# Retention and feed-forward block: the states gathered right behind the scores, their share added right behind the own values, into other PSUM banks

## The reference, cut to what matters

```python
xn = _layernorm(x)
# attention: 8 heads of 16, chunks of 64 tokens, in every chunk
attn = einsum('bhid,bhjd->bhij', qc, kc) * D          # D: causal, with decay
o_intra = einsum('bhij,bhje->bhie', attn, vc)         # a block's own values
o_inter = einsum('bhid,bhde->bhie', qc * decay_q, S)  # the states' share
S_new = decay_s * S + einsum('bhjd,bhje->bhde', kc * decay_k, vc)
# feed forward: ternary weights and a low-rank part
h = _bitlinear(xn, w_fc) + gate * (xn @ v.T @ fast_b.T @ u.T)
r = maximum(h, 0)
out = x + o @ Wo + _bitlinear(r * r, w_proj)
```

## Time and profile before

| | us |
|---|---|
| median of 3 runs | 129.81 |
| lowest, highest | 127.7, 129.81 |
| the profiled execution's own time | 129.01 |
| its span, first to last instruction | 127.0 |
| outside the span | 2.0 |
| PE busy | 117.0 (92%) |
| DVE busy | 99.2 (78%) |
| ACT busy | 78.7 (62%) |
| POOL busy | 64.0 (50%) |

### The profile page before, as it was taken

The page is one execution under the profiler, slowest core; times in us unless marked ns, Lnnn a source line. Parts: engine busy times, 40 slices in busy tenths (PEclk is TensorE's granted clock), DMA queues, the critical chain, the costliest instruction groups (busy, mean ns, idle before and its releaser), DMA issues.

```text
span 127.0 us, 6564 instructions
## 1 busy us (share of the span) xinstructions
PE 117.0 (92%) x2860; PEld 92.8 (73%) x2860; DVE 99.2 (78%) x261; ACT 78.7 (62%) x158; POOL 64.0 (50%) x60
## 2 busy tenths in 40 slices
PE   4979999988999999499999999999999999499991
PEld 4425869856688778377788778878897889377890
DVE  0788795489799969858699979896999799729832
ACT  3265669967871897227972897188738774382910
POOL 7099803984439161923439252916193529544400
PEclk9999999999999999999999999999999999999998
DMA  3849920000023000400023001300020002000202
GB/s 105 296 149 320 389 92 34 0 3 5 8 90 81 5 0 23 145 7 0 0 92 74 0 0 53 112 0 0 0 83 0 0 0 83 0 5 0 88 5 83
DMA packets 3357, 7.71 MB, mean 61 GB/s; under 512 B 384, under 2 KB 896, under 8 KB 3216
## 3 DMA queue, kind: packets, MB, share of 16 engines
q1 hardware_dynamic: 2880, 7.01, 16.3%
q10 hardware_dynamic: 464, 0.50, 1.2%
HBM read 5.42 MB, written 2.10 MB: 59 GB/s over the span
## 4 chain that ended last, share of the span: by engine, by line
PE 80%; DVE 10%; issue 4%; ACT 2%; POOL 1%; DVEq 0%; POOLq 0%
PE ps_work L659 10%; PE ps_score L735 8%; PE ps_work L663 7%; PE ps_work L660 7%; PE ps_score L705 6%; PE ps_score L747 5%; PE ps_score L781 5%; PE ps_y L761 4%; PE ps_y L762 4%; PE ps_score L720 3%; DVE sums_of L532 3%; PE ps_turn L668 3%; PE ps_y L765 2%; DVE xn L491 2%; PE ps_turn L692 1%
## 5 line engine op out<-in xcount | busy, mean ns | idle before, releaser
L300 POOL TENSOR_TENSOR sq_lo<-square,sq_hi 128x512 fp32r<-128x512 f32 x31 | 39.8, 1295 | 36.2 <-ACT sq_hi L356 36.2
L347 ACT ACTIVATE square<-ps_work 128x512 f32<-128x512 f32 x32 | 19.1, 596 | 23.1 <-PE ps_work L663 22.6
L516 DVE TENSOR_TENSOR scores<-ps_score,cst 128x512 f32<-128x512 f32 x32 | 20.3, 682 | 1.6 <-PE ps_score L705 1.6
L305 POOL TENSOR_TENSOR q_pair<-q_dec,cst 128x1024 f32<-128x1024 f32 x7 | 13.3, 1894 | 15.9 <-DVE q_dec L501 15.9
L356 ACT ACTIVATE sq_hi<-square 128x512 fp32r<-128x512 f32 x32 | 20.1, 627 | 0.1
L352 ACT ACTIVATE square<-square 128x512 f32<-128x512 f32 x32 | 18.9, 630 | 0.1
L491 DVE TENSOR_SCALAR xn<-x_in,mean_var,rstd 128x128 f32<-128x128 f32 x32 | 14.9, 528 | 0.3
L659 PE MATMUL ps_work<-xn_hi,w_hi 128*128 128x512 f32 x32 | 14.3, 447 | 0.4 <-issue 0.4
L735 PE MATMUL ps_score<-scores,v_pad 64*32 64x64 f32 x1024 | 12.5, 225 | 1.6 <-issue 1.6
L663 PE MATMUL ps_work<-xn_lo,w_hi 128*128 128x512 f32 x32 | 12.6, 394 | 0.0
L660 PE MATMUL ps_work<-xn_hi,w_lo 128*128 128x512 f32 x32 | 12.6, 393 | 0.0
(11 more groups left out here) (123 smaller groups left out, 238.6 us busy)
## 6 DMA issues: line engine op xcount, KB each, us to landing
x_in<-x_tok SPq DMA_DIRECT2D x8, 256.0 KB, 3.4
resid<-x_feat SPq DMA_DIRECT2D x1, 2048.0 KB, 7.7
out_feat<-resid SPq DMA_DIRECT2D x7, 256.0 KB
po_in<-ffn_weights SPq DMA_DIRECT2D x1, 320.0 KB, 3.2
fc_in<-ffn_weights SPq DMA_DIRECT2D x1, 256.0 KB, 3.7
q_table<-q_decay SPq DMA_DIRECT2D x1, 256.0 KB, 3.5
wqvk<-qvk_weights ACTq DMA_DIRECT2D x1, 192.0 KB, 3.9
cst<-const ACTq DMA_DIRECT2D x1, 129.0 KB, 3.9
```

Source lines behind the costliest of these rows:

```text
L300: nc.gpsimd.tensor_tensor(sq_lo[p][:, f, :], square[p][:, f, :], sq_hi[p][:, f, :].bitcast(F32), ALU.subtract).then_inc(lo_ready, 1)
L347: nc.scalar.activation(square[b.parity][:, f, :], ps_work[f % 2][:], ACT.Relu).then_inc(relu_ready, 1)
L516: nc.vector.tensor_tensor(scores[:, g].rearrange("p t s i -> p (t s) i"), ps_score[:, g].rearrange("p (a i) -> p a i", i=BLK), causal.unsq ...
```

## The change

- The banks `ps_turn` and `ps_y` become one tensor `ps_both`, and `gather_states` writes its states there (row block r to bank r) and not to banks 2 and 3 of `ps_score`. It waits no longer for masks, and stands right behind `score`. So `take_states` must have read `ps_both` before the transposes of the next batch (`turn_xn`) write there.
- `carry(b)` moves to the end of its own batch's pass, right behind `own_values(b)`.
- `hidden` runs tiles 0, 1 and 2, then scores and states, then tile 3. `second_product(before)` moves behind the transposes.
- VectorE: `low_o(before)` comes first; the masks are taken in order, with `take_states` behind the first; the three adds stand behind `low_xn` and ahead of `finish(before)`. The statistics of the batch after next are made at the end of a pass.
- ScalarE: `high_o(before)` first, other order of relu, square and rounded square, the root of the batch after next last. GpSimd: the four subtractions in a row, then `spread_q`.
- In the last batch the subtraction of the fourth tile goes from VectorE to GpSimd.
- `place_program` adds tiny products on small tiles: 40 at the start in place of 12, 9 ahead of the first `carry`, 20 ahead of the last own values in place of 6. Of the three wide products at the start one and a half are left.

The diff, cut to its core:

```diff
+        ps_both = pb("ps_both", [P, ROWS, SEQ])
+        ps_turn, ps_y = ps_both[:, 0, :], ps_both[:, 1, :]
+        w1_bank = ps_score[:, NG - 1, :]
...
             def body(b):
-                for f in range(2):
+                for f in range(NF):
                     low_square(b, f)
                 spread_q(b.step(1))
-                for f in range(2, NF):
-                    low_square(b, f)
...
-            def body(b):
+            def body(b, more):
+                high_o(b.step(-1))
                 take_relu(b, 0)
                 take_relu(b, 1)
-                root(b.step(1))
+                take_relu(b, 2)
                 take_square(b, 0)
+                high_square(b, 0)
                 take_square(b, 1)
-                high_square(b, 0)
-                high_o(b.step(-1))
-                take_relu(b, 2)
+                take_relu(b, 3)
+                round_xn(b.step(1))
                 high_square(b, 1)
-                round_xn(b.step(1))
-                take_relu(b, 3)
                 take_square(b, 2)
+                high_square(b, 2)
                 take_square(b, 3)
-                high_square(b, 2)
+                high_square(b, 3)
                 copy_k(b.step(1))
                 copy_k_tok(b.step(1), 0)
-                high_square(b, 3)
                 copy_k_tok(b.step(1), 1)
+                if more:
+                    root(b.step(2))
...
-            def body(b):
-                before, after = b.step(-1), b.step(1)
-                statistics(after)
-                statistics_done(after)
-                take_states(before)
-                variance(after)
-                for k in range(3):
-                    add_states(before, k)
+            def body(b, more):
+                before, after, later = b.step(-1), b.step(1), b.step(2)
+                low_o(before)
                 for step in range(4):
                     inverse_root(after, step)
                 normalise(after)
-                low_o(before)
+                mask_scores(b, 0)
+                take_states(b)
+                for g in range(1, NG):
+                    mask_scores(b, g)
                 low_xn(after)
-                for g in MASK_ORDER[:2]:
-                    mask_scores(b, g)
+                for k in range(3):
+                    add_states(b, k)
                 finish(before, ps_y)
                 decay_q(after)
...
             def turn_xn(b, before=None):
                 pe.wait_ge(xn_ready, b.count(1, 1))
+                if before is not None:
+
+                    pe.wait_ge(state_step, before.count(3, 1))
...
-                pe.wait_ge(scores_ready, b.count(NG, ROWS))
+                pe.wait_ge(v_ready, b.count(2, 2))
...
-                            ins = mm(ps_score[g * GW:(g + 1) * GW, ROWS + r, t * GW:(t + 1) * GW],
+                            ins = mm(ps_both[g * GW:(g + 1) * GW, r, t * GW:(t + 1) * GW],
...
+            def hidden_and_scores(b):
 
                 pe.wait_ge(q_ready, b.count(1, 1))
                 hidden(b, 0)
                 pe.wait_ge(k_ready, b.count(1, 1))
                 hidden(b, 1)
+                hidden(b, 2)
+                pe.wait_ge(o_lo_ready, b.count(1, 0))
+                score(b)
+                gather_states(b)
+                hidden(b, 3)
+
+            def body(b):
+                before, after = b.step(-1), b.step(1)
+                hidden_and_scores(b)
+                turn_xn(after, b)
                 second_product(before, ps_y, range(NF))
-                carry(before)
-                hidden(b, 2)
-                hidden(b, 3)
-                turn_xn(after)
-                pe.wait_ge(o_lo_ready, before.count(1, 1))
-                score(b)
                 output_product(before, ps_y)
                 project_q(after, b)
                 project_k(after, b)
                 project_vk(after, 0)
                 project_vk(after, 1)
-                gather_states(b)
                 own_values(b)
+                carry(b)
```

More of the change, by code:

```diff
@@ L85, in over_batches, with over_middle @@
         body(Batch(half, 2))
+def over_middle(engine, body):
+    with engine.Fori(0, NB // 2 - 2) as half:
+        body(Batch(half, 1), True)
+        body(Batch(half, 2), True)
+    body(Batch(NB // 2 - 2, 1), True)
+    body(Batch(NB // 2 - 2, 2), False)
 def build(nc, x_tok, x_feat, qvk_weights, ffn_weights, rank_weights, const, q_decay, out_feat):
@@ L586, in _ @@
             normalise(after)
-            for g in MASK_ORDER:
-                mask_scores(first, g)
             dve.wait_ge(proj_step, 1)
@@ L594, in _ @@
             nc.vector.tensor_scalar(wo_scaled[:], wo_in, inv_scale2[:], None, ALU.mult).then_inc(wo_ready, 1)
+            mask_scores(first, 0)
+            take_states(first)
+            mask_scores(first, 1)
+            mask_scores(first, 2)
             low_xn(after)
+            mask_scores(first, 3)
             decay_q(after)
@@ L683, in project_vk @@
             def project_vk(b, side):
-                if side == 1 and b is first:
-                    pe.wait_ge(q_ready, b.count(1, 1))
-                elif side == 1:
+                if side == 1 and b is not first:
                     pe.wait_ge(y_free, b.count(1, 0))
@@ L803, in _ @@
             project_vk(first, 1)
-            score(first)
-            after = first.step(1)
-            pe.wait_ge(v_ready, 2)
-            pe.wait_ge(w1_split, 1)
-            for f in range(NF):
-                hidden(first, f)
-            turn_xn(after)
+            after = first.step(1)
+            pe.wait_ge(q_ready, 1)
+            pe.wait_ge(w1_split, 1)
+            hidden(first, 0)
+            pe.wait_ge(k_ready, 1)
+            hidden(first, 1)
+            hidden(first, 2)
+            score(first)
+            gather_states(first)
+            hidden(first, 3)
+            turn_xn(after, first)
             pe.wait_ge(proj_ready, 1)
@@ L816, in _ @@
             ins.then_inc(proj_turned, 1)
-            gather_states(first)
-            own_values(first)
+            project_q(after, first)
             pe.wait_ge(wo_ready, 1)
@@ L821, in _ @@
             nc.tensor.transpose(ps_y[:, 0:D], wo_scaled[:], ident).then_inc(wo_turned, 1)
-            project_q(after, first)
             project_k(after, first)
@@ L825, in _ @@
             project_vk(after, 1)
-            def body(b):
-                before, after = b.step(-1), b.step(1)
+            own_values(first)
+            place_program(9, ps_score[:, NG - 1, :], ident)
+            carry(first)
+            def hidden_and_scores(b):
                 pe.wait_ge(q_ready, b.count(1, 1))
```

139 lines of the change are left out of this document (64 added, 75 removed).

## The result

The changed kernel takes 149.8 us (median of 4 runs, 149.4 to 152.5), the kernel before 129.6 us beside it. The ratio is 1.164, with a 95% interval of 1.150 to 1.179. It is slower, as forecast, but by 20 us where the forecast had 9: 139.1 us, range 132 to 142.

What follows compares the result with a forecast made beforehand. TensorE was taken to bound the kernel, with a new 2.0 us wait in each pass. Span 127.0 + 2.0 (start) + 9.8 (six passes) - 1.7 (last batch) = 137.1, plus 2.0 outside: 139.1 us, range 132 to 142.

Steps and rivals of the forecast that it cites:

- what bounds the changed kernel: Each pass: TensorE waits 2.0 us ahead of the fourth pair of products by token, for adds delayed by three subtractions; 0.58.
- T: Start of hidden tile 0 in a pass, from which the forecast counts its times; next pass at T+13.2 without other waits.
- the lock: VectorE's adds on the states: one that meets a running GpSimd subtraction waits for its end, 1.2 to 1.4 us each.
- The rivals with two subtractions: Adds in a pass: only two subtractions are waited for, the wait is 1.0 us, time 133.1 us; chance 0.14.
- no wait: Products by token: adds end before T+9.3, TensorE does not wait, time 126.7 us; chance 0.21 with little wait included.
- no gain from the moved tiles: States right behind scores on TensorE: one refill and entry saved, at most 0.2 us a pass, cancelled by 0.16 back.
- +2.0, from 1.2 to 2.6: Start: carry of batch 0 ahead of the loop +0.91, nine tiny products 0.3 to 0.7, waits 0 to 1.0 us.
- The unnamed idle of 1.64 I keep as 1.6: Six passes: TensorE's idle stretch without a named cause stays at 1.6 us, possibly elsewhere; it can be 0 to 4.
- the idle stretches grow: Rows of small tiles on TensorE: 4 us of unnamed idle in place of 1.6, time 141.5 us; chance 0.07.
- for 92.8: Six passes of 15.2 us, 91.2, together with 1.6 of unnamed idle, against 82.97 before: +9.8 us.
- for 17.4: Last batch to the end of the span: 17.4 us, with 0.4 of waiting, where it took 19.1 before: -1.7.
- the twenty tiny products, put at 1.5 us: Last batch, ahead of the own values: twenty tiny products cost 0.7 to 1.5 us, taken as 1.5.

Runs made afterwards that it cites:

- The first experiment: Changed kernel with GpSimd's second subtraction of a pass made to wait for take_states and the three adds: 137.8 us, ratio 1.071 to the kernel before.
- the best version: Changed kernel with GpSimd's wait, 12 tiny and three wide products at the start, a wide one behind the first transposes, 6 later tiny products for 29: 131.6 us.
- the filler: One wide product of zeros ahead of the first projection, in TensorE's 0.78 us pause; two versions of the changed kernel differing in it alone: 135.5 us without, 131.6 with.
- the wide warm-up: Changed kernel with GpSimd's wait and three wide products at the start in place of one and a half: 135.2 us, ratio 1.037 to the kernel before.
- the filled start: Changed kernel with GpSimd's wait, three wide products at the start and one more wide product behind the first transposes: 133.1 us, ratio 1.032 to the kernel before.

## Why the forecast had the sign and not the size

**Right: what bounds the changed kernel.** In the sixth pass, which no other idle time disturbs, T is 116.10. The adds ask at T+7.17 (forecast T+7.12) and end at T+11.34 (11.26), `finish` ends at T+12.00 (12.03), and side 1 starts at T+12.05 (12.1) where its place in the order was T+10.17 (10.12). The adds take 1.39 each there, and the pass 15.27 (15.2). GpSimd took its turn ahead of the third add, as the earlier trace rows had it. The first experiment took 12.0 us away with the lock, the price that the working had for it (within the 9 to 15 that the intervals leave). The rivals with two subtractions (133.1) or no wait (126.7) are out.

**Right, and small: no gain from the moved tiles.** These are the scores and states of the sixth pass:

```profile
118.66 1.21 PE L722 MATMUL ps_score<-q_pair,k_feat 32*64 32x128 f32 x64
119.80 0.69 PE L737 MATMUL ps_both<-v_pad,k_tok 64*32 64x32 f32 x56
```

The states begin 1.14 us behind the scores where 1.06 was reckoned, and carry 1.41 behind the own values where it was 1.30. So a change between kinds of small tiles costs about 0.1 us, as a refill does. That agrees with the rule of the Trainium skill, TensorEngine Tiling (Array Packing), Key Properties, that a change of mode drains the engine. By the rule a pass without a wait would be 0.2 longer than in the sum. Here 0.08 of it stands ahead of the wait for the residual, which swallows it, and the pass was 0.07 longer.

**Wrong: the start.** The step "+2.0, from 1.2 to 2.6" should have been +8.4 (33.31 for 24.91). What it costed, the work that the change moves there, was about right: the best version, with 12 tiny and three wide products, the filler and without the nine tiny products, begins its first pass at 28.03 us, 1.00 of it an "issue" stretch, so the moved work is 2.1 over the kernel before, and the nine tiny products are 0.3. What failed is that the step passed over the warm-up as if 40 tiny products and one and a half wide ones did what 12 and three did. TensorE was idle for 1.87 us at 6.4 us, then ran batch 0's products 0.43 us apart instead of 0.23 until 19.2 us. With three wide products and the filler the scores of batch 0 came 3.8 us earlier (17.98 for 21.74), and with 12 tiny ones for 40 another 0.8 (17.22). The remaining 1.4 are an "issue" stretch of 0.94 and a wait of 0.50 for the last add.

**Wrong: the idle stretches.** The step "The unnamed idle of 1.64 I keep as 1.6" had 0 to 4 as its bounds. There were 5.8 us, of which 2.3 in the passes, 0.94 at the start and 2.51 in the last batch. The rival "the idle stretches grow" had the right mechanism with 0.07 of the chance and 2.4 us of price; a change that adds 100 products to a program (2,960 for 2,860 in the count of the trace) whose only long stretch lay in a row of small tiles had to be priced by the number of such places, not by the one seen.

**Missing: the clock.** No term allowed for TensorE at its lower level. In the profiled execution it was there from 63.6 to 70.4 and from 97.7 to 101.1 us:

```profile
97.18 1.85 PE L752 MATMUL ps_score<-scores,v_pad 64*32 64x64 f32 x128
98.96 1.72 PE L764 MATMUL ps_score<-q_dec,sums_of 32*32 32x64 f32 x56
100.60 0.73 PE L675 MATMUL ps_work<-xn_hi,w_hi 128*128 128x512 f32 x1
```

Carry takes 0.98 in the row at full clock (124.09 above), 1.72 here. What TensorE did before it fell: it had waited for the residual for 1.7 us each time, until 1.6 and 1.5 us before the fall (62.01 and 96.27). The same wait in the other four passes had no fall behind it, so the one idle stretch is not enough to foretell it.

**The sum again.** The span was 150.3 for 137.1, 13.2 more: start 6.4, six passes 5.3, last batch 1.5. The passes took 98.06 us for 92.8: 0.4 from the pass itself, 0.7 because the idle in them was 2.3 and not 1.6, and 4.1 nearly all in the passes in which the clock was at half (the second to the fifth). The last batch took 18.93 for 17.4, with the 2.51 of idle in it. Without that it would be 1.0 shorter than forecast, so here two errors partly met: the twenty tiny products, put at 1.5 us, took 0.43 (139.11 to 139.54).

**Where the 20 us went, from the runs.** 149.8, then 137.8 without the lock, 135.2 with the wide warm-up, 133.1 with the filled start, 131.6 with fewer tiny products, and 129.8 for the kernel before. The lock is 12 us and the start some 5; the rest, some 3, is left to the number and places of the products and the idle stretches, and no run separates it further. The first step and the sum of the next two are clear of the noise, but the single steps from 137.8 to 135.2 and to 133.1 are not.

## What to carry to other kernels

When an instruction with two inputs in SBUF on VectorE moves beside GpSimd's work, price it at GpSimd's duration, then look at what stands behind it on VectorE and who waits for that; reordering moves the price, and only a wait or another place takes it away. When a change adds or moves many small products, count them: find where the long "issue" stretches stand in the count, and ask whether rows of small tiles now begin more than some 90 products ahead of such a place. Look at the clock behind a warm-up and not only at the warm-up: here wide products alone did not keep it in the new order, and wide products with the pause behind them filled did. And 28 one-column products that seem free cost the kernel before 15 us, 5.5 of it at the start.

## What was not expected of the hardware

- TensorE stops inside rows of small tiles, or right behind one, for 0.5 to 2.9 us, only at places about 126 products apart, and goes on 1.0 to 1.6 us behind the end of a 16 KB packet of instructions (50 of 50 cases). It happens where a part of the program is run for the first time: behind place 1099 (batch 2) no version shows one of over 0.4 us until the last batch, though the passes between repeat the same rows of small tiles.
- A small amount of idle time costs more than itself: behind an idle stretch the granted clock can be at half for 3.4 us, in which carry takes 1.71 instead of 0.98.
- GpSimd pays little for the lock: in one pass (75.95 us) its three subtractions took 4.09 us together beside the adds, and 3.78 behind them. VectorE pays nearly all, 4.18 for 1.23.
- Tiny products cost 0.015 us each in the count when they go round the four row groups (80 in 1.17 us), and 0.054 when they write one tile (80 in 4.35 us).
